# Two seven-product units per pair of row blocks instead of one, in an attention kernel on one Trainium2 core

## What is computed

```python
h = relu(layernorm(x))                                # 4096 x 512
q, k, v = h @ Wq.T + bq, key @ Wk.T + bk, value @ Wv.T + bv
s = (q @ k.T) / 64 * adj                              # 4096 x 4096
s = where(abs(s) < 1e-5, -1e9, s)
out = x + softmax(s) @ v @ Wm.T + bm
```

## Time and profile before

| | |
|---|---|
| median of three runs | 1566.84 us |
| the profiled execution, its own time | 1566.73 us |
| its span in the profile | 1564.9 us |
| TensorE busy | 1541.6 us (99%) |
| VectorE busy | 1105.6 us (71%) |
| ScalarE busy | 625.0 us (40%) |
| mean share of the DMA engines | 67% in a steady pass |
| chain that ended last, TensorE's part | 90% |

### The profile page before, as it was taken

How to read it: one execution, slowest core, us unless ns; L and a number is a source line. 1 busy time by engine, 2 the same in 40 slices (tenths; PEclk the granted TensorE clock), 3 DMA queues, 4 the chain that set the end, 5 groups by cost and what they waited for, 6 DMA issues and landing times.

```text
span 1564.9 us, 24177 instructions
## 1 busy us (share of the span) xinstructions
PE 1541.6 (99%) x7134; PEld 707.1 (45%) x7134; DVE 1105.6 (71%) x2444; ACT 625.0 (40%) x1009; POOL 223.4 (14%) x285
## 2 busy tenths in 40 slices
PE   8998999999999999999999999999999999999998
PEld 5543444444444444444444444444444444444444
DVE  5989887767667676767767666776766667676652
ACT  5776343333334333343333333433333333333332
POOL 5162002011020101102010010201001020200100
PEclk9999999999999999999999999999999999999999
DMA  9824768667675765758576575766658576665754
GB/s 347 272 75 99 180 153 204 165 153 178 141 201 141 181 162 145 189 134 203 145 179 167 130 203 133 201 147 173 165 131 207 130 202 151 163 165 141 185 112 108
DMA packets 449149, 260.60 MB, mean 167 GB/s; under 512 B 376531, under 2 KB 380883, under 8 KB 448982
## 3 DMA queue, kind: packets, MB, share of 16 engines
q1 hardware_dynamic: 449104, 260.12, 66.6%
q10 hardware_dynamic: 6, 0.01, 0.0%
HBM read 156.51 MB, written 12.06 MB: 108 GB/s over the span
## 4 chain that ended last, share of the span: by engine, by line
PE 90%; DVE 5%; issue 2%; DMA 1%; ACT 1%; SPq 0%; DVEq 0%; ACTq 0%
PE R L738 14%; PE R L740 14%; PE R L739 14%; PE S L740 11%; PE S L738 11%; PE S L739 11%; PE M L738 3%; PE M L740 3%; PE M L739 3%; DMA pT<-ph 1%; DVE Zbuf L1550 1%; PE R L809 1%; DVE Zbuf L1472 1%; PE R L855 1%; DVE small L1226 1%
## 5 line engine op out<-in xcount | busy, mean ns | idle before, releaser
L1177 ACT ACTIVATE drop<-Zbuf 128x512 f32<-128x512 f32 x256 | 161.2, 630 | 737.8 <-DVE cmx L1472 644.2
L738 PE MATMUL R<-Vbuf,pT 128*128 128x512 f16 x1008 | 382.1, 379 | 7.4 <-DMA pT<-ph 4.9
L740 PE MATMUL R<-Vbuf,pT 128*128 128x512 f16 x1008 | 382.0, 379 | 0.0
L739 PE MATMUL R<-Vbuf,pT 128*128 128x512 f16 x1008 | 382.0, 379 | 0.0
L738 PE MATMUL S<-Kbuf,qT 128*128 128x512 f16 x856 | 324.5, 379 | 0.0
L739 PE MATMUL S<-Kbuf,qT 128*128 128x512 f16 x856 | 324.4, 379 | 0.0
L740 PE MATMUL S<-Kbuf,qT 128*128 128x512 f16 x856 | 324.4, 379 | 0.0
L1519 DVE SCALAR_TENSOR_TENSOR Zbuf<-S,rs,adjb 128x512 f32<-128x512 f32 x214 | 160.2, 749 | 217.6 <-PE S L740 211.9
L1472 DVE CUSTOM_DVE_ANT_0 Zbuf<-drop,Zbuf 128x512 f32<-128x512 f32 x256 | 190.5, 744 | 0.0
L1572 DVE TENSOR_SCALAR drop<-drop,rs 128x512 f32<-128x512 f32 x256 | 145.9, 570 | 27.2 <-ACT drop L1177 25.0
L1183 ACT ACTIVATE Zbuf<-Zbuf,smx 128x1024 f32<-128x1024 f32 x128 | 157.4, 1230 | 5.3 <-DVE smx L1486 2.5
(11 more groups left out here) (251 smaller groups left out, 1628.6 us busy)
## 6 DMA issues: line engine op xcount, KB each, us to landing
adjb<-in_adj_dram SPq DMA_DIRECT2D x256, 256.0 KB, 2.9
Kbuf<-key_factors SPq DMA_DIRECT2D x98, 512.0 KB, 4.0
xq<-in_x_dram SPq DMA_DIRECT2D x32, 256.0 KB, 2.8
Kbuf<-in_L_gnn_key_dram SPq DMA_DIRECT2D x8, 1024.0 KB, 13.6
xr<-in_x_dram SPq DMA_DIRECT2D x32, 256.0 KB, 2.7
out_dram<-xr SPq DMA_DIRECT2D x31, 256.0 KB, 2.5
Vbuf<-in_L_gnn_value_dram SPq DMA_DIRECT2D x7, 1024.0 KB, 7.4
pT<-ph SPq DMA_TRANSPOSE x130, 3.2
```

Source lines behind the costliest of these rows:

```text
L738: nc.tensor.matmul(ps, lhs[0], rhs[0], start=start, stop=False, skip_group_check=added)
L739: nc.tensor.matmul(ps, lhs[0], rhs[1], start=False, stop=False, skip_group_check=added)
L740: return nc.tensor.matmul(ps, lhs[1], rhs[0], start=False, stop=stop, skip_group_check=added)
L1177: nc.scalar.activation(drop[:, :], tile_of(s.i, s.j), ACT.Abs).then_inc(abs_ready, 1)
```

## The change

Two units, of key groups (5, 4) and (7, 6), replace the one. Their first two tiles each are steps 4, 5 and 6, 7 of the first block; in the second block their tiles alternate with ordinary ones (steps 8, 10, 12, 14 of units, 9, 11, 13, 15 ordinary). The probabilities of the second block are taken in an order of their own (`SECOND_PROBS`), so that the slots in which the next sums are kept come free early. Four factors stay in SBUF (`kept`), ten are loaded in each pass into three slots; the mixes lie in an eighth slot. The units run from pass 3 (`FIRST` is 4, and passes 0 to 3 are unrolled). Factor making has 16 pieces, steps t = 19 to 50. Row preparation is moved: projection and row scaling to c = 7, scaling units to j = 0 and 12, q's split to j = 0 and 9; `row_mixes` to j = 1, their high half to j = 2, their low half to j = 3.

The hunks on `load_factor` are SP's: those for j = 5 to 9 stand at the head of its step, ahead of the adj load, the last two at its end, behind the transpose. `row_mixes` stands ahead of the bias addition of c = 2 in POOL's step, where it stood behind it. The next hunk is ScalarE's, the last one VectorE's.

```diff
-        FACTORS = ["B11", "B21", "B22", "T1", "T2", "T3", "T4"]
+        UNITS = [(5, 4), (7, 6)]
+        FACTORS = [(w, f) for w in range(len(UNITS)) for f in ("B11", "B21", "B22", "T1", "T2", "T3", "T4")]
...
-        FIRST_ORDER, SECOND_ORDER = [0, 1, 2, 3, 4, 5, 7, 6], [6, 7, 0, 1, 2, 3, 4, 5]
-        ONE, TWO = 7, 6
+        FIRST_ORDER, SECOND_ORDER = [0, 1, 2, 3, 5, 4, 7, 6], [4, 0, 5, 1, 6, 2, 7, 3]
+        SECOND_PROBS = [4, 5, 6, 7, 0, 1, 2, 3]
+        UNIT, NU, MAKE_STEP, FIRST = 4, len(UNITS), 19, 4
+        RING_Q, MIX_Q = (4, 5, 6), 7
...
-        qS = Zbuf[:, 1, 0:2 * CW].bitcast(fp16).rearrange("p (h s n) -> p h s n", h=2, s=2 * ND)
+        qS = ring_slot(MIX_Q).rearrange("p (h s n) -> p h s n", h=2, s=2 * ND)
-        PIECES = [(t, s) for s in range(2) for t in CHAIN]
+        PIECES = [(w, t, s) for w in range(NU) for s in range(2) for t in CHAIN]
...
+                self.stats = row_at(0, self.c == 5)
+                self.halves_h = row_at(1, self.c == 6)
+                self.turned = row_at(2, self.c == 7)
+                self.projected = row_at(3, self.c == 7)
+                self.scaled = row_at(4, j in (0, NC + 4))
+                self.halves_q = row_at(5, j in (0, NC + 1))
...
-                self.strassen = self.has_scores and (not fixed or i >= 2)
-                self.unit = j - UNIT if self.strassen and UNIT <= j < UNIT + 4 else None
+                self.strassen = self.has_scores and (not fixed or i >= FIRST - 1)
+                self.unit, self.w = None, 0
+                if self.strassen and UNIT <= j < NC:
+                    self.w, self.unit = (j - UNIT) // 2, (j - UNIT) % 2
+                elif self.strassen and j >= NC and j % 2 == 0:
+                    self.w, self.unit = (j - NC) // 4, 2 + (j - NC) // 2 % 2
...
+                if s.strassen and s.j == 5:
+                    wait(sp, scores_done, s.t)
+                    load_factor((1, "B21"), 4)
+                if s.strassen and s.j == 6:
+                    wait(sp, unit_mm, 6 * s.nth + 3)
+                    load_factor((1, "T1"), 5)
+                    wait(sp, scores_done, s.t)
+                    load_factor((1, "B22"), 6)
+                if s.strassen and s.j == 7:
                     sp.wait_ge(kt_stored, 16 * 2 * len(PIECES))
+                    wait(sp, scores_done, s.t)
+                    load_factor((0, "T3"), 4)
+                if s.strassen and s.j == 8:
+                    wait(sp, scores_done, s.t)
+                    load_factor((1, "T3"), 6)
+                if s.strassen and s.j == 9:
+                    wait(sp, scores_done, s.t)
+                    load_factor((1, "T4"), 4)
...
+                if s.strassen and s.j == 7:
+                    wait(sp, unit_mm, 6 * s.nth + 6)
+                    load_factor((0, "T4"), 5)
+                if s.prefetch and s.j in (13, 14, 15):
+                    wait(sp, scores_done, s.t)
+                    load_factor((0, ("T1", "B22", "B21")[s.j - 13]), (5, 6, 4)[s.j - 13])
...
+                if s.strassen and s.j == 1:
+                    row_mixes(s.i)
...
                 if s.unit == 0:
-                    wait(act, unit_mm, s.unit_before + 1)
-                    wait(act, s_made, s.i - 1)
-                    nc.scalar.activation(SUM_U, S[s.j % 2][:, :], ACT.Copy).then_inc(p1_ready, 1)
+                    wait(act, unit_mm, 6 * s.nth + 3 * s.w + 1)
+                    wait(act, p_lo, PASS * (s.i - 1) + NC + 2 * s.w + 2)
+                    nc.scalar.activation(SUM_U[s.w], S[s.j % 2][:, :], ACT.Copy).then_inc(p1_ready, 1)
...
-                if s.strassen and s.j == 5:
-                    wait(dve, s_hi, s.i - 1)
+                if s.strassen and s.j == 3:
+                    wait(dve, s_hi, s.nth + 1)
```

More of the change, by code:

```diff
@@ L356, in __init__, with row_at @@
                 self.i = i
[L357 to L368, removed]
+                def row_at(stage, steady):
+                    if fixed and self.t < 21:
+                        found = [n + 1 for n in HEAD if HEAD[n][stage] == self.t]
+                        return found[0] if found else None
+                    if not steady:
+                        return None
+                    n = self.b + (3 if self.c >= 5 else 2)
+                    return n if not late or n <= NB else None
+                self.stats = row_at(0, self.c == 5)
[4 more added lines that the diff above has]
+                self.halves_q = row_at(5, j in (0, NC + 1))
                 self.has_next = not late or b + 1 < NB
@@ L372, in __init__ @@
                 self.more_adj = not late or t + ADJ_SLOTS < STEPS
-                self.more_x = not late or self.pb + 1 < NB
+                self.more_x = self.halves_q is not None and (not late or self.halves_q < NB)
                 self.pair = NPAIR * 2 * i + (j - LAG_P) // 2
@@ L671, in row_mixes @@
             def row_mixes(i):
+                nth = i - (FIRST - 1)
                 wait(pool, q_in, 16 * (2 * i + 1))
-                wait(pool, p_lo, PASS * (i - 1) + NC + 2)
-                for p, full in enumerate((FULL_1, FULL_2)):
+                wait(pool, p_lo, PASS * (i - 1) + NC)
+                for p, full in enumerate(FULLS):
                     hi, lo = [qT[:, p, h, :, :].rearrange("p s n -> p (s n)") for h in range(2)]
@@ L727, in step @@
                     nc.gpsimd.tensor_tensor(xr[:, :], xr[:, :], obias[:, :], ALU.add).then_inc(xr_ready, 1)
-                if s.strassen and s.j == 3:
-                    row_mixes(s.i)
             run(pool, step)
@@ L992, in step @@
                     last.then_inc(pv_done, 1)
-                if s.pc == 3 and s.has_prep:
+                if s.projected is not None:
                     if isinstance(s.t, int) and s.t < NC:
@@ L1207, in step @@
                     nc.scalar.activation(row[:, 0, :], O[s.p][:, :], ACT.Copy, scale=rsum[:, 2:3]).then_inc(o_hi, 1)
-                if s.splits_q and s.has_prep:
-                    wait(act, q_scaled, s.n)
-                    wait(act, h_in, 16 * (s.n - 1))
+                if s.halves_q is not None:
+                    wait(act, q_scaled, s.halves_q)
+                    wait(act, h_in, 16 * (s.halves_q - 1))
                     nc.scalar.activation(row[:, 0, :], xq[:, :], ACT.Copy).then_inc(q_hi, 1)
@@ L1540, in step @@
                         nc.vector.tensor_reduce(wmax[:, 4:5], vsum[:, :], X, ALU.max).then_inc(part_max, 1)
-                if s.pc == 0 and s.has_prep:
-                    row_stats(s.n)
+                if s.stats is not None:
+                    row_stats(s.stats)
                 if s.has_P:
@@ L1569, in step @@
                     wait(dve, abs_ready, s.t + 1)
-                    if s.pc == 0 and s.has_prep:
-                        wait(dve, bn_ready, s.n)
+                    if s.stats is not None:
+                        wait(dve, bn_ready, s.stats)
                     nc.vector.tensor_scalar(drop[:, :], drop[:, :], rs[:, r, 1, s.g // 2:s.g // 2 + 1], rs[:, r, 2, s.g // 2:s.g // 2 + 1], ALU.is_lt, ALU.mult)\
```

233 lines of the change are left out of this document (122 added, 111 removed).

## The result

The median of 11 runs of the changed kernel is 1569.18 us (1567.39 to 1571.23), against 1565.37 for the kernel before on the same chip (1564.01 to 1566.91): a ratio of 1.0025, with a 95% interval of 1.0015 to 1.0034. The change makes the kernel slower by a quarter of a per cent. The forecast had 1558.6 and faster. The profiled execution took 1568.17, its span 1566.3; that of before took 1566.73.

A forecast was written before the change was run, and what follows sets the result against it. TensorE, busy in 99% of the span, bounds the kernel. A pass: -1.52 + 0.6 + 0.3 = -0.62, thirteen -8.1; 1566.73 + 1.07 - 8.1 - 1.1 = 1558.6 us, range 1549 to 1569.

The forecast's parts named there:

- Matmuls removed: Steady passes: 420 matmuls at 0.2158 us make 90.65, 1.52 under 92.17 if nothing waits; 13 passes gain.
- the wait of step 4: First unit, step 4: third product waits 0.6 us a pass for ScalarE's product copy, queued behind its output-row copy.
- L1550 and its wait: Low half of the row mixes, moved from step 5 to 3: its 0.23 us TensorE wait per pass goes, within the 1.52.
- Vector work: VectorE in steady passes: a further unit adds 3.2 us, making 68 of 91; hidden, priced at nothing.
- loads: Ten factors a pass instead of seven: DMA share some 0.74; the second unit's B21 tightest, cost 0 to 0.7 a pass.
- values: Step 10's values, after the moved projection and row scaling: transpose may land late, cost 0 to 0.8 a pass.
- mixes: POOL's row mixes moved from step 3 to 1, bias addition behind them: cost 0 to 1.1 a pass, nearest 0.1.
- Rival (d): Step 3: POOL's bias addition L727 holds VectorE's maximum, 1.9 us of waits a pass, 1571.6, slower; chance 0.12.
- Making factors: Start, up to step 50: pieces double from 8 to 16; priced at 0, one late landing 0 to 5.4 once.
- The last pass: Step 9 becomes ordinary, putting 6 matmuls ahead of its values and removing the transpose wait: -1.1 us.

The follow-up runs named there:

- the best version: Changed kernel with projection late while factors are made, factor halves at the step's end, first product copied before the output row: 1550.37 us, ratio 0.9903.

## Why the prediction was wrong

**Matmuls removed: right.** 7062 matmuls, at the pitch of 0.2158. Busy time fell by 12.6, and the 1.52 a pass holds: once the wait of step 4 is gone a steady pass takes the 90.65 that was worked out.

**L1550 and its wait: right.** L1599, as it is now called, starts 1.88 after step 3's read (worked out: 1.86), and no steady pass waits for it.

**Step 4: right.** VectorE, ScalarE and TensorE of the changed kernel there:

```profile
453.12 0.75 DVE L1567 SCALAR_TENSOR_TENSOR Zbuf<-S,rs,adjb 128x512 f32<-128x512 f32 x1 [1.48 <-PE S L779]
453.79 0.68 DVE L1519 CUSTOM_DVE_ANT_0 Zbuf<-drop,Zbuf 128x512 f32<-128x512 f32 x1
...
455.00 1.22 DVE L1599 TENSOR_TENSOR Kbuf<-Zbuf,Kbuf 128x1024 f16<-128x1024 f32 x1
```

```profile
457.30 0.69 ACT L1254 ACTIVATE row<-R,small 128x512 f16<-128x512 f32 x1 [2.09 <-DVE small L1657]
457.88 0.59 ACT L1190 ACTIVATE Zbuf<-S 128x512 f32<-128x512 f32 x1
```

```profile
457.73 0.38 PE L779 MATMUL R<-Kbuf 128*128 128x512 f16 x1
458.53 0.39 PE L777 MATMUL S<-Kbuf,qT 128*128 128x512 f16 x1 [0.42 <-ACT Zbuf L1190]
```

Counted from 453.12 the output-row copy starts at 4.18 (4.17 worked out) and the product's copy at 4.76 (4.75). The matmul behind it starts 0.58 beyond the pitch (0.6). Taking the copies in the other order removes it.

**Vector work, loads, values, mixes in steady passes: right that they cost little, a bit high.** I took 0.3 a pass for the last three together, and about 0.1 was there: eight of eleven passes take 90.65 + 0.58, and three another 0.13 to 0.43 for a late transpose. VectorE has 67 of 91 (68 worked out), and the DMA share is 0.74 to 0.76 (0.74).

**Rival (d): didn't happen, by a third of a microsecond.** The bias addition on POOL in step 3:

```profile
452.19 1.27 POOL L769 TENSOR_TENSOR xr<-xr,obias 128x512 f32<-128x512 f32 x1
```

It ends at 453.46 and the maximum (L1519) starts at 453.79 and takes its usual 0.68. The 1.76 of the earlier trace rows was beside such an addition. The Trainium skill (SBUF — State Buffer, Who interferes with whom) has the two excluding each other only while they overlap; with no overlap here, the 0.68 agrees. Nothing of the slowdown is this rival's: its "slower" came true, its mechanism didn't.

**Making factors: the step that failed.** I wrote "nothing for the next" of the pass that makes most factors, since PE was busy 92.20 of 92.20 there. The number was right and the inference wrong. A busy TensorE says that the chains behind it had some slack, not how much, and I never measured it. ScalarE was already waiting up to 5.4 us for a store in the kernel before, and 4.12 for the counterpart of the one above, hidden by the 4 us between the transposed h and its use:

```profile
227.01 0.38 ACT L1162 ACTIVATE early<-R 128x256 f16<-128x256 f32 x1 [4.12 <-DMA key_factors<-early]
```

The change spends that slack twice, with the projection a step earlier and with more stores in the queue (three more raw factors, and halves up to step 50). I priced the earlier projection in the steady passes alone. Measured: 12.4 us, against 0. The run with the projection late shows that its place is the cause of the waits for h up to 345 us. In steps 48 to 51 it isn't (gaps of 5.1 with the projection late, 3.9 in the changed kernel), and there the halves at the end of a step take 2.5 to 2.7 away.

**The last pass: half right.** The wait for step 9's transpose went (1.1), but one for step 10's came, behind two factor loads and a store in SP's queue, with no projection there to cover it:

```profile
1489.45 0.68 SPq L497 DMA_DIRECT2D Kbuf<-key_factors  x1
1490.18 0.43 SPq L625 DMA_DIRECT2D out_dram<-xr  x1
1490.65 0.43 SPq L497 DMA_DIRECT2D Kbuf<-key_factors  x1
1491.20 0.37 SPq L481 DMA_DIRECT2D adjb<-in_adj_dram  x1
1492.46 1.44 SPq L558 DMA_TRANSPOSE pT<-osb  x1
```

The values that read it start at 1498.06, 5.6 after the issue and 1.36 late. So this stretch lost 0.3 where I had it gain 1.1.

**The ledger.** To the forecast of 1558.6 come 12.4 for the start and 1.4 for the last pass. Off it go 0.24 x 13 = 3.1 for the steady passes, and 1.0 for a transpose wait at 172 us that shrank from 1.66 to 0.62 (scatter: it was 1.26 and 0.34 in the runs with the projection late and with the copy first, whose code is the same up to there). That makes 1568.3, against 1568.17 profiled. The range missed the median by only 0.2, and that is luck: its upper end took in dearer steady passes, and the whole allowance for the start was "one late landing is 0 to 5.4 once", of which the sum took 0.

**What stays open.** Why some waits of TensorE are followed by half-rate matmuls and others of like length aren't (below). How much of the start's loss the three further stores of raw factors bring. What the best version's last 2.6 us at steps 48 to 51 hang on was not tried, nor was a second buffer for the halves, which would take the store out of the chain.

## What to carry to other kernels

When a step of a hand-made order moves, price it in every phase that runs that order, the start above all: a busy bound engine doesn't show slack, so measure for each moved step the time between a producer's landing and its use, and add up what the change takes from it. A wait that is taken out of one in-order queue can turn up in the next queue that holds both its producer and your consumer; follow it through all of them, the DMA-issuing queue included. And a schedule can be chosen by phase: late where factors are made, early after, was worth 7 us alone and 19 with two reorderings.

## What the runs showed of the hardware

After some waits of TensorE the matmuls come 0.427 us apart for a while, at a granted clock of 0.50, the 1.2 GHz level. Eight of them, the usual number here, cost 1.7 us more. They followed waits of 3.16 in the changed kernel, 2.78 with the projection late, 2.52 with the halves last, 2.86, 3.12 and 2.18 with the copy first, and 3.86 with the later stores (13 of them, 2.6 us). They didn't follow waits of 2.24 and 2.28 in the changed kernel, 2.57 with the halves last, 3.42 and 2.97 in the version with all edits and the later stores. In the run with the copy first, three or four matmuls ran at full pace behind the wait before the slow ones. So in these runs the length of a wait doesn't decide alone whether the clock falls.

The landing of a transpose isn't a constant. In the changed kernel its median is 3.3, and 5.6 for the one of the last pass, with two factor loads of 0.5 MB, a store and an adj load issued in the 3 us ahead of it. The same transpose behind the same four took 5.2 in the best version and 6.8 in the one with the later store on top. With one of the two loads moved behind it, it took 3.9.
